# Six layers of local attention: projections in three float32r passes, split weights from the second attention, another order of scores, half copies and a third value buffer

## The chip, the core and the metric

One core of a Trainium2 chip runs one launch of a program that computes a whole four-block network. TensorE (PE, with its weight loads as PEld), VectorE (DVE), ScalarE (ACT), GpSimd (POOL) and SyncE (SP, which here only issues transfers) run their own instruction streams and meet through semaphores. The time is device microseconds of one execution; shown is the median of three runs.

## The reference, cut to what matters

The residual `x` (2048 tokens of 128 features, held with the features on the partitions) passes four blocks, each an attention-like part and a feed-forward part on a normalised copy. The change concerns the feed-forward part of the third block, which is itself a network of six layers. Each layer is:

```python
x = attn_layer(shift_tokens(x), Wqkv[i], q_scale[i], k_scale[i], Wo[i]) + x
x = ffn_layer(shift_tokens(x), ln_g[i], ln_b[i], W1[i], b1[i], W2[i], b2[i]) + x
# attn_layer: 16 heads of 64; attention in windows of 32 tokens, each with the window before it
qkv = x @ Wqkv                       # 128 -> 3 * 1024
q = l2norm(q) * qs ; k = l2norm(k) * ksc      # then rotary tables
out = local_attention(q, k, v) ; return out @ Wo
```

## The kernel before, in words

The program runs stage after stage: block 0 (names b0...), the second attention `b1a` (relative positions; function `attend`), its feed-forward `b1f`, the small attention `b2a`, then the six layers, `b2f` (functions `block2_ffn` and `layers_of_attention`), and block 3 (`b3...`). Between stages all engines meet at a barrier.

In `b2f` the 2048 tokens are 16 tiles of 128 tokens, and six layers make 96 tiles. One loop of steps is written by hand on every engine; step `s` works on four tiles at once. PE does, in this order: the projections of queries and keys of tile `s` (`project_qk`, L2356), the turning of the attention output of tile `s-3` (L2371, `b2f_o_rows`), of the keys and then of the queries of tile `s-1` (L2371), the output product of tile `s-3` (`output`, L2378), the turning of the probabilities of tile `s-2` (L2371, `b2f_prob`), the scores of tile `s-1` (`scores`, L2387 and 128 small products at L2393), the value projection of tile `s` (`project_v`, L2365), a piece of the feed-forward of an earlier quarter (`feed`), and the weighing of the values of tile `s-2` (`weigh_values`, 128 small products at L2406). The feed-forward of a quarter (four tiles) is cut into six phases, one a step, so that steps come in rounds of four. They are called here A (phase 2, L2428), B (phase 3, the three gate products, L2436), C (phases 4 and 0, L2442 and L2417) and D (phases 5 and 1, L2447 and L2422). In steps B the scores stand behind the gate products, directly ahead of the weighing:

```python
gates = any(phase == 3 for f, phase in feed_forward(s))
if not gates and 0 <= s - 1 < n_tiles:
    scores(s - 1, here)
if s < n_tiles:
    project_v(s)
feed(s, range(6))
if gates and 0 <= s - 1 < n_tiles:
    scores(s - 1, here)
if 0 <= s - 2 < n_tiles:
    weigh_values(s - 2, other)
```

ACT copies what PE turned (`b2f_o_cols` L2565, `b2f_kt` L2572, `b2f_qt` L2574, `b2f_pt` L2581), squares queries and keys (`square`, L2527), copies the values (`b2f_v_rows` L2586), does the gelu of the gates in steps B (L2554) and 16 exponentials of 64 columns (L2536). DVE rotates, reduces, normalises the keys (L2649) and scales. POOL adds the rotated parts (L2293, L2296) and takes powers for the lengths (L2303). SP moves the values of a tile across partitions in 16 transfers (L2271 to L2279), behind the weighing of the tile two before it, and in the ninth tile of each layer loads all weights of the next layer into the other of two buffers (L2262). ACT may write the values of a tile into one of two buffers once the transfers of the tile before are done. The projections are float32 products, which stand in a trace as two records each; all of the layer's weights, `b2f_wqkv` among them, come from the inputs.

In `b1a` (`attend`) 16 groups of 8 steps run; ACT copies position scores (L1733) and exponentiates (L1725), SP writes them to a scratch tensor in HBM and reads them back skewed, POOL makes two shifted copies of the keys for each group (L1557).

Of the kernel before, what the change touches and what calls it, by code (L numbers as in the profile page):

```python
# [16 lines left out]
P = 128  # L17
# [557 lines left out]
def block0_ffn(nc, K, w, xn, x):  # L575

    with ExitStack() as ctx:
# [3 lines left out]
        rounded = rounded_constants(M, "b0f", K.pick16, None)  # L581
        parts = two_parts(M, "b0f_xn", [P, N])
        with ExitStack() as inner:
# [3 lines left out]
            to_rows(nc, K, "b0f", probs, ROUTED0, gates, K.pick16[:], rounded)  # L587
# [179 lines left out]
def block0_weights(M, W):  # L767
# [8 lines left out]
              f_router=later("b0f_router", [P, ROUTED0]))  # L776
# [3 lines left out]
def block0_attn(nc, K, weights, xn, x, fetch):  # L780

    with ExitStack() as ctx:
# [18 lines left out]
        with ExitStack() as inner:  # L801
# [4 lines left out]
            rounded = rounded_constants(I, "b0m", K.pick4, 1)  # L806
            parts = two_parts(I, "b0m_flat", [P, N])
            with ExitStack() as rt:
# [3 lines left out]
                to_rows(nc, K, "b0m", probs, 4, gates, K.pick4[:], rounded, b2)  # L812
# [199 lines left out]
def block1_ffn(nc, K, W, w, xn, x, fetch):  # L1012

    with ExitStack() as ctx:
# [7 lines left out]
        rounded = rounded_constants(M, "b1f", K.pick8, 1)  # L1022
        parts = two_parts(M, "b1f_xn", [P, N])
        with ExitStack() as rt:
# [4 lines left out]
            to_rows(nc, K, "b1f", probs, EXPERTS1, gates, K.pick8[:], rounded, b2)  # L1029
# [12 lines left out]
def block2_weights(M, W):  # L1042
# [6 lines left out]
              wqkv=two("wqkv", 3 * INNER), wo=two("wo", PAIRS, P), w1=two("w1", 6, P), w2=two("w2", 3, P),  # L1049
              small=two("small", 9), scales=two("scales", 4, HD2), turn=two("turn", QT, 4, HD2))  # L1050
    return w, first.pairs + layer_weights(W, w, 0)


def layer_weights(W, w, l):
# [3 lines left out]
            ((w.wqkv, of("b2f_wqkv")), (w.turn, W["c_rotary2"]), (w.scales, of("b2f_scales")),  # L1058
# [172 lines left out]
def head_attention(nc, K, W, weights, key, xn, x, relative, fetch=()):  # L1231
# [3 lines left out]
    with ExitStack() as ctx:  # L1235
# [11 lines left out]
        attend(nc, K, key, q_op, k_op, extra, ident, values, table, unseen, merged, relative, fetch)  # L1247
# [179 lines left out]
def attend(nc, K, key, q_op, k_op, extra, ident, values, table, unseen, merged, relative,  # L1427
           fetch):

# [56 lines left out]
    with ExitStack() as ctx:  # L1486
# [13 lines left out]
        if relative:  # L1500
            e_sb = M.sb(f"{key}_e_sb", [P, RING, 2, QW])
            band = M.sb(f"{key}_band", [P, BANDS, 2, BAND])
            e_ps = M.ps(f"{key}_e_ps", [P, QW])
            scratch = K.scratch
        shift_parts = shift_cols[:].rearrange("p t (h c) -> p (t h) c", h=2)[
            :, :, SHIFT_AT:SHIFT_AT + 3 * kinds].rearrange("p n (k r) -> p n k r", r=3)
        with stage(nc, "queries_even", "queries_odd", "keys_even", "keys_odd", "k_kinds", "e_ready", "e_copied",
# [3 lines left out]
                   "merged", "fetched", "dve_chain") as (block, S):  # L1511
# [38 lines left out]
            def _(pool):  # L1550
                if relative:
                    for g in range(GROUPS):
# [162 lines left out]
            def _(act):  # L1715
# [24 lines left out]

                for i in ticks:
                    s, a = i - LAG, i + E_LEAD
                    if 0 <= s < STEPS:
# [7 lines left out]
                    if to_copy_out(i) is not None:  # L1751
                        copy_outputs(to_copy_out(i))

# [423 lines left out]
QK_SCALE = 8.0  # L2177


def block2_ffn(nc, K, W, w, xn, x):  # L2180

    with ExitStack() as ctx:
# [3 lines left out]
        G = Names(  # L2186
            xs=one("xs", B * SEQ), ms=one("ms", B * SEQ),
# [9 lines left out]
            v_rows=two("v_rows", 2, QW), values=two("values", WINS, QW),  # L2197
# [13 lines left out]
def layers_of_attention(nc, K, W, G, Z, xn, x):  # L2211
# [7 lines left out]
    LOADS = 7  # L2219
# [16 lines left out]
    with stage(nc, "began", "weights_even", "weights_odd", "moved_even", "moved_odd",  # L2236
# [6 lines left out]
               "stored", "x_added", "dve_chain") as (block, S):  # L2243
# [11 lines left out]
        def _(sp):  # L2255
# [9 lines left out]
            for g in range(n_tiles):  # L2265
# [770 lines left out]
```

## Time and profile before

| | us |
|---|---|
| runs shown | 3986.25, 3980.16, 3975.45 (median 3980.16) |
| the profiled execution | 3985.77, span 3984.0 from the first to the last instruction |
| PE busy | 3442.9 (86%) |
| DVE, ACT, POOL busy | 2975.4 (75%), 2435.9 (61%), 1397.3 (35%) |
| DMA | 72 GB/s over the span |
| products L2356 of `b2f`, first to last start | 1480.8 to 3232.7 |

A row of the trace is an instruction or a run of like ones: start, length, engine, line, operation, what it writes and reads, shape and count, and in brackets the idle time of the engine before it with what ended it. "issue" means that nothing in the profile explains the wait. A PE row's length counts the fill of the array, so a product's cost is the distance between starts.

### The profile page before, as it was taken

How to read it: one execution, taken by the hardware profiler on the slowest of the kernel's cores; microseconds unless marked ns; L12 is line 12 of the kernel's file. 1: busy time of each engine (PE TensorE's matmuls, PEld its weight loads, DVE VectorE, ACT ScalarE, POOL GpSimd, SP SyncE). 2: the span in 40 equal slices, each digit the busy share in tenths (PEclk: the TensorE clock that was granted, in tenths of full speed). 3: DMA queues.
4: the chain of work that ended last, by engine and by line, in shares of the span. 5: the costliest groups of instructions: out<-in, count | busy, mean ns of one | idle time of the engine just before them, and what ended most of it. 6: DMA issues, size and time to landing. Idle time of an engine off the chain costs nothing. (4 is left out here: it accounts for less than half of the span.)

```text
span 3984.0 us, 102916 instructions
## 1 busy us (share of the span) xinstructions
PE 3442.9 (86%) x40985; PEld 2125.3 (53%) x40985; DVE 2975.4 (75%) x5754; ACT 2435.9 (61%) x4558; POOL 1397.3 (35%) x641
## 2 busy tenths in 40 slices
PE   5668768888859958999999999999999986999898
PEld 3356623333338826666666666666666663222785
DVE  6957657777649868778778778778778755887585
ACT  3436437777728826676676676676676652455573
POOL 4820011111100007666666666666666640000000
PEclk8879859999969979999999999999999997899899
DMA  1000057777511002322322322322322211100000
GB/s 41 0 12 1 14 189 226 232 230 229 179 35 46 11 2 68 100 56 62 97 56 63 96 58 60 97 56 63 96 57 61 59 44 59 35 22 16 13 17 11
DMA packets 174807, 285.80 MB, mean 72 GB/s; under 512 B 36979, under 2 KB 76916, under 8 KB 172404
## 3 DMA queue, kind: packets, MB, share of 16 engines
q1 hardware_dynamic: 173748, 278.48, 23.9%
q8 instruction: 327, 5.36, 0.6%
q14 instruction: 156, 1.28, 0.1%
q10 hardware_dynamic: 576, 0.69, 0.1%
HBM read 104.05 MB, written 74.45 MB: 45 GB/s over the span
## 5 line engine op out<-in xcount | busy, mean ns | idle before, releaser
L2303 POOL TENSOR_TENSOR b2f_norm<-b2f_norm,b2f_minus_half 128x16 f32<-128x16 f32 x192 | 554.8, 2909 | 276.1 <-DVE b2f_norm L2644 276.1
L2293 POOL TENSOR_TENSOR b2f_q<-b2f_q,b2f_q_part 128x1024 f32<-128x1024 f32 x96 | 228.2, 2377 | 656.2 <-DVE b2f_q_part L2634 656.2
L1725 ACT ACTIVATE b1a_weights<-b1a_b_ps 128x512 f32<-128x512 f32 x512 | 278.0, 598 | 39.6 <-PE b1a_b_ps L1650 36.1
L2586 ACT ACTIVATE b2f_v_rows<-b2f_q_ps 128x1024 f32<-128x1024 f32 x96 | 98.4, 1025 | 265.6 <-PE b2f_q_ps L2365 137.5
L1840 DVE TENSOR_REDUCE b1a_tops<-b1a_a_ps 128x1 f32<-128x512 f32 (+3 forms) x512 | 244.8, 502 | 19.7 <-PE b1a_a_ps L1606 18.2
L1557 POOL TENSOR_SCALAR b1a_k_op<-b1a_k_op,b1a_extra 128x1024 bf16<-128x1024 bf16 x32 | 90.6, 2843 | 448.6 <-DMA b1a_k_op<-part_copies 410.3
L1725 ACT ACTIVATE b3a_weights<-b3a_b_ps 128x512 f32<-128x512 f32 (+3 forms) x384 | 161.7, 505 | 136.3 <-PE b3a_b_ps L1660 135.2
L2643 DVE TENSOR_REDUCE b2f_norm<-xn 128x16 f32<-128x1024 f32 x192 | 234.3, 1220 | 13.6 <-ACT xn L2527 5.8
L2536 ACT ACTIVATE b2f_prob<-b2f_odd_ps,b2f_bias,b2f_norm 128x64 f32<-128x64 f32 x768 | 233.2, 443 | 7.5 <-DVE b2f_bias L2660 6.3
L2536 ACT ACTIVATE b2f_prob<-b2f_even_ps,b2f_bias,b2f_norm 128x64 f32<-128x64 f32 x768 | 233.3, 449 | 2.3 <-DVE b2f_bias L2660 2.3
L1733 ACT ACTIVATE b1a_e_sb<-b1a_e_ps 128x512 f32<-128x512 f32 x256 | 153.2, 599 | 123.5 <-PE b1a_e_ps L1592 120.1
L2296 POOL TENSOR_TENSOR b2f_k<-b2f_k,b2f_k_part 128x1024 f32<-128x1024 f32 x96 | 227.4, 2369 | 1.0 <-DVE b2f_k_part L2634 1.0
L2356 PE MATMUL b2f_q_ps<-b2f_wqkv,b2f_xs 128*128 128x512 f32 x384 | 215.4, 688 | 8.1 <-DVE b2f_kt L2610 5.7
L1835 DVE CUSTOM_DVE_ANT_0 b1a_summed<-b1a_a_ps,b1a_band 128x256 f32<-128x256 f32 (+2 forms) x320 | 142.5, 445 | 96.5 <-PE b1a_a_ps L1606 94.5
L2378 PE MATMUL b2f_q_ps<-b2f_o_cols,b2f_wo 128*128 128x128 f32 x1536 | 192.1, 279 | 3.4 <-ACT b2f_o_cols L2565 2.2
L2365 PE MATMUL b2f_q_ps<-b2f_wqkv,b2f_xs 128*128 128x512 f32 x384 | 189.8, 617 | 1.6 <-ACT xn L2527 1.6
L2356 PE MATMUL b2f_k_ps<-b2f_wqkv,b2f_xs 128*128 128x512 f32 x384 | 184.5, 603 | 0.0
L2378 PEld LDWEIGHTS b2f_q_ps<-b2f_o_cols,b2f_wo 128*128 128x128 f32 x1536 | 180.3, 193 | 5.7 <-ACT b2f_o_cols L2565 2.9
L1606 PE MATMUL b1a_a_ps<-b1a_k_op,b1a_q_op 64*128 64x512 bf16 x512 | 139.8, 406 | 23.3 <-DVE b1a_tops L1840 22.9
L2630 DVE TENSOR_TENSOR b2f_q<-b2f_q_ps,b2f_turn 128x1024 f32<-128x1024 f32 x96 | 117.3, 1222 | 51.9 <-PE b2f_q_ps L2356 44.5
L694 POOL TENSOR_TENSOR b0s_drive<-b0s_raw,xn 128x1024 f32<-128x1024 f32 x32 | 135.5, 4233 | 52.0 <-DVE b0s_raw L709 52.0
L2565 ACT ACTIVATE b2f_o_cols<-b2f_even_ps 128x1024 f32<-128x1024 f32 x48 | 49.2, 1026 | 153.8 <-PE b2f_even_ps L2371 153.6
(519 smaller groups left out, 9246.7 us busy)
## 6 DMA issues: line engine op xcount, KB each, us to landing
b2f_values<-b2f_v_rows SPq DMA_DIRECT2D x1534, 64.0 KB
position_scratch<-b1a_e_sb SPq DMA_DIRECT2D x128, 512.0 KB, 3.9
b1a_band<-position_scratch SPq DMA_DIRECT2D x128, 384.0 KB
b2f_wqkv<-in_b2f_wqkv SPq DMA_DIRECT2D x6, 1536.0 KB, 8.2
b2f_turn<-in_c_rotary SPq DMA_DIRECT2D x6, 1024.0 KB, 8.4
b1f_raw<-in_b1f_both SPq DMA_DIRECT2D x9, 512.0 KB, 3.5
part_copies<-b1a_parts SPq DMA_DIRECT2D x12, 256.0 KB
b2f_wo<-in_b2f_wo SPq DMA_DIRECT2D x6, 512.0 KB, 9.7
```

Of the source, the lines that this page charges most:

```text
L1725: act.activation(weights[:, s % P_RING, c, lo:QW], b_room(s, c)[:, lo:QW], ACT.Exp).then_inc(S.exps_ready, 1)
L1733: act.activation(e_sb[:, a % RING, h], e_ps[:], ACT.Copy).then_inc(S.e_copied, 1)
L1835: ins = dve.tensor_tensor_reduce(summed[:, n % 4, 0:z1 - z0], src, band[:, a % BANDS, h, at0:at0 + z1 - z0], 1.0, LOWEST, ALU.add, ALU.max ...
L1840: ins = dve.tensor_reduce(out, src, AX_X, ALU.max)
L2293: pool.tensor_tensor(G.q[:, g % 2], G.q[:, g % 2], G.q_part[:], ALU.add) \
L2296: pool.tensor_tensor(G.k[:, g % 2], G.k[:, g % 2], G.k_part[:], ALU.add) \
L2303: pool.tensor_tensor(part, part, G.minus_half[:, 0:HEADS], ALU.pow) \
L2356: pe.matmul((Z.q, Z.k)[j // 2][:, j % 2], tile_input(g), G.wqkv[:, l % 2, cols(j, QW)], start=True, stop=True).then_inc(S.qk_ready, 1)
L2365: ins = pe.matmul(Z.q[:, h], tile_input(g), wv[:, :, h], start=True, stop=True)
L2378: ins = pe.matmul(Z.q[:, 0, 0:P], G.wo[:, layer(g) % 2, p], G.o_cols[:, p], start=(p == 0), stop=(p == PAIRS - 1))
L2536: act.activation(G.prob[:, i // 2, i % 2], ps[:, i % 2, cols(i // 2, HD2)], ACT.Exp, bias=G.bias[:, i:i + 1], scale=G.norm[:, g % 3, i:i + ...
L2643: chain(dve.tensor_reduce(norm[:, cols(i, HEADS)], G.squares[:, i], AX_X, ALU.add))
```

## The change

In `b2f` each projection becomes three float32r products, head by head, tail by head and head by tail, of inputs and weights that are split into a rounded head and the rest. POOL splits each input tile two steps ahead (`split_tile`). The weights are split beforehand in `b1a`: ACT loads half a layer's weights, POOL splits it, ACT stores both parts to HBM (`wqkv_parts`), 12 halves in the first 12 groups. `b2f_wqkv` now has one buffer with head and tail; the keys' and queries' columns of the next layer are loaded when the last tile of a layer is projected, the values' columns behind that tile's moves. In steps B the scores go ahead of the gate products. The copy of `b2f_o_cols` is made in two halves, each half of the queries' turning waiting for its own half. The values get three buffers. The constants for picking experts are loaded later, with the weights of the blocks that use them.

```diff
-            wqkv=two("wqkv", 3 * INNER), ...
+            wqkv=M.sb("b2f_wqkv", [P, 2, 3 * INNER], F32R), ...
+def projection_weights(K, w, l, lo, hi):
+    return [(w.wqkv[:, part, lo:hi].bitcast(F32), K.wqkv_parts[l, part, :, lo:hi]) for part in range(2)]
...
+                        if g < 2 * LAYERS:
+                            pool.wait_ge((S.raw_even, S.raw_odd)[g % 2], 16 * (g // 2 + 1))
+                            if g:
+                                pool.wait_ge(S.raw_stored, 32 * g)
+                            pool.tensor_copy(raw_parts.head[:], raw[:, g % 2]).then_inc(S.raw_headed, 1)
+                            pool.wait_ge(S.raw_headed, g + 1)
+                            pool.tensor_tensor(raw_parts.tail[:], raw[:, g % 2], raw_parts.head[:].bitcast(F32),
+                                               ALU.subtract).then_inc(S.raw_tailed, 1)
...
                 for i in ticks:
+                    if i >= 0 and i % QT == QT - 1 and i // QT < halves:
+                        store_half(i // QT)
+                        if i // QT + 2 < halves:
+                            load_half(i // QT + 2)
...
             for g in range(n_tiles):
+                ends = g % TILES == TILES - 1 and layer(g) + 1 < LAYERS
+                if ends:
+                    sp.wait_ge(S.qk_ready, 4 * g + 4)
+                    for dst, src in projection_weights(K, G, layer(g) + 1, 0, 2 * INNER):
+                        sp.dma_start(dst, src).then_inc(S.keys_loaded, 16)
                 sp.wait_ge(S.v_copied, g + 1)
...
+                if ends:
+                    for dst, src in projection_weights(K, G, layer(g) + 1, 2 * INNER, 3 * INNER):
+                        sp.dma_start(dst, src).then_inc(S.values_loaded, 16)
...
+            def split_tile(g):
+                l, at = layer(g), at_column(g % TILES)
+                if l:
+                    pool.wait_ge(S.stored, 2 * (g // per_q - QUARTERS + 1))
+                if g >= X_RING:
+                    pool.wait_ge(S.v_ready, g - X_RING + 1)
+                head, tail = (G.x_parts[:, g % X_RING, part] for part in range(2))
+                pool.tensor_copy(head, G.xs[:, at:at + P]).then_inc(S.x_headed, 1)
+                pool.wait_ge(S.x_headed, g + 1)
+                pool.tensor_tensor(tail, G.xs[:, at:at + P], head.bitcast(F32), ALU.subtract) \
+                    .then_inc(S.x_tailed, 1)
...
+            def project(g, ps, weights):
+                head, tail = (G.x_parts[:, g % X_RING, part] for part in range(2))
+                for n, (a, b) in enumerate(((head, 0), (tail, 0), (head, 1))):
+                    ins = pe.matmul(ps, a, weights(b), start=(n == 0), stop=(n == 2))
...
+                    if l:
+                        pe.wait_ge(S.keys_loaded, 16 * PROJECTION_LOADS * l)
+                if g % TILES == 0 and layer(g):
+                    pe.wait_ge(S.values_loaded, 16 * PROJECTION_LOADS * layer(g))
...
-                feed(s, range(6))
                 if gates and 0 <= s - 1 < n_tiles:
                     scores(s - 1, here)
+                feed(s, range(6))
...
-                    act.activation(G.o_cols[:], pairs(here), ACT.Copy).then_inc(S.o_copied, 1)
+                    for j in range(2):
+                        act.activation(G.o_cols[:, 4 * j:4 * j + 4],
+                                       here[:, j].rearrange("p (c n) -> p c n", n=P), ACT.Copy) \
+                            .then_inc(S.o_copied, 1)
...
-                    if s >= 1:
-                        act.wait_ge(moved[(s - 1) % 2], moved_until(s - 1))
+                    if s >= 2:
+                        act.wait_ge(moved[s % 2], moved_until(s - 2))
```

The order of PE in the end of the first step B of `b2f` before (the first row is the turning of the probabilities, the last two rows begin step C):

```order
L2371 MATMUL b2f_even_ps<-c_ident,b2f_prob 128x128 x8
L2365 MATMUL b2f_q_ps<-b2f_wqkv,b2f_xs 128x512 x2
L2436 MATMUL b2f_k_ps<-b2f_normed,b2f_w 128x512 x2
L2436 MATMUL b2f_q_ps<-b2f_normed,b2f_w 128x512
L2387 MATMUL b2f_odd_ps<-b2f_mask,b2f_ident 128x512 x2
L2393 MATMUL b2f_odd_ps<-b2f_kt,b2f_qt 32x64 x64
L2406 MATMUL b2f_even_ps<-b2f_values,b2f_pt 32x64 x64
L2356 MATMUL b2f_q_ps<-b2f_wqkv,b2f_xs 128x512 x2
L2356 MATMUL b2f_k_ps<-b2f_wqkv,b2f_xs 128x512 x2
```

The scores (L2393) and the weighing (L2406) were neighbours. The same place of the changed program, on PE again:

```order
L2450 MATMUL b2f_even_ps<-c_ident,b2f_prob 128x128 x8
L2415 MATMUL b2f_q_ps<-b2f_wqkv,b2f_x_parts 128x512 x6
L2466 MATMUL b2f_odd_ps<-b2f_mask,b2f_ident 128x512 x2
L2472 MATMUL b2f_odd_ps<-b2f_kt,b2f_qt 32x64 x64
L2515 MATMUL b2f_k_ps<-b2f_normed,b2f_w 128x512 x2
L2515 MATMUL b2f_q_ps<-b2f_normed,b2f_w 128x512
L2485 MATMUL b2f_even_ps<-b2f_values,b2f_pt 32x64 x64
L2415 MATMUL b2f_q_ps<-b2f_wqkv,b2f_x_parts 128x512 x6
L2415 MATMUL b2f_k_ps<-b2f_wqkv,b2f_x_parts 128x512 x6
```

The three gate products (L2515) now lie between the scores (L2472) and the weighing (L2485), and two projections are six products.

The transfers that SP issues where the first layer ends, in the changed program: the last two moves of tile 14, then the first moves of tile 15 (in the program before nothing stands between them):

```order
L2322 DMA b2f_values<-b2f_v_rows 32x512
L2326 DMA b2f_values<-b2f_v_rows 32x512
L2316 DMA b2f_wqkv<-wqkv_parts 128x2048 x2
L2322 DMA b2f_values<-b2f_v_rows 32x512
L2330 DMA b2f_values<-b2f_v_rows 32x512
```

The load of the keys' and queries' columns stands behind all moves of tile 14; that of the values' columns (L2335, 128x1024 x2) stands likewise behind all 16 moves of tile 15.

ACT in `b1a`, at the end of the second group, in the changed program (L1744 are exponentials, L1752 copies of position scores):

```order
L1744 ACTIVATE b1a_weights<-b1a_b_ps 128x512 x2
L1752 ACTIVATE b1a_e_sb<-b1a_e_ps 128x512
L1769 DMA wqkv_parts<-b1a_raw_head 128x1536
L1769 DMA wqkv_parts<-b1a_raw_tail 128x1536
L1763 DMA b1a_raw<-in_b2f_wqkv 128x1536
```

Three issues a group came in between the two, in the last step of each of the groups 0 to 9; groups 10 and 11 have the two stores alone, and two loads stand ahead of the first step.

## Rows read from the trace of the kernel before

**Rows 1.** Windows: a layer of b2f; 400 us of b1a (clock, DMA share, GB/s last).

```profile
2350.00:2650.00 300.00, 280.05 (x5247) 191.12 (x5233) 232.77 (x325) 204.22 (x394) 193.20 (x93) 0.98 0.27 71
589.00:989.00 400.00, 356.95 (x2597) 130.20 (x2597) 302.24 (x1030) 306.88 (x580) 67.97 (x24) 0.99 0.72 232
```

**Rows 2.** Timeline of PE in b2f, one round of steps A, B, C, D.

```profile
2350.09 1.98 PE L2356 MATMUL b2f_q_ps<-b2f_wqkv,b2f_xs 128*128 128x512 f32 x4
...
2353.63 1.04 PE L2371 MATMUL b2f_even_ps<-c_ident,b2f_o_rows 128*128 128x128 f32 x8
...
2355.88 1.06 PE L2371 MATMUL b2f_even_ps<-c_ident,b2f_q 128*128 128x128 f32 x8 [0.33 <-ACT b2f_o_cols L2565]
2357.20 2.05 PE L2378 MATMUL b2f_q_ps<-b2f_o_cols,b2f_wo 128*128 128x128 f32 x16 [0.26 <-ACT xn L2527]
...
2362.00 1.98 PE L2365 MATMUL b2f_q_ps<-b2f_wqkv,b2f_xs 128*128 128x512 f32 x4
...
2366.22 1.98 PE L2356 MATMUL b2f_q_ps<-b2f_wqkv,b2f_xs 128*128 128x512 f32 x4
...
2382.96 1.46 PE L2406 MATMUL b2f_even_ps<-b2f_values,b2f_pt 64*32 64x64 f32 x126
2386.68 0.37 PE L2406 MATMUL b2f_even_ps<-b2f_values,b2f_pt 64*32 64x64 f32 x2 [2.26 <-issue]
2386.98 3.33 PE L2356 MATMUL b2f_q_ps<-b2f_wqkv,b2f_xs 128*128 128x512 f32 x4
...
2406.91 1.98 PE L2356 MATMUL b2f_q_ps<-b2f_wqkv,b2f_xs 128*128 128x512 f32 x4
...
2425.49 0.70 PE L2356 MATMUL b2f_q_ps<-b2f_wqkv,b2f_xs 128*128 128x512 f32 x1
```

**Rows 3.** Waits of PE over all of b2f, the longest in total.

```profile
PE b2f_even_ps L2406 <- issue: 54.9, 24, 4.9
```

**Rows 4.** DMA queues in the stretch 2383.9 to 2385.3.

```profile
q8 instruction: 1, 0.02, 5.4%
```

**Rows 5.** Windows: the beginning of that step C (granted clock third from last).

```profile
2386.30:2389.70 3.40, 3.02 (x5) 1.29 (x5) 1.29 (x2) 3.15 (x11) 0.00 (x0) 0.50 0.19 48
```

**Rows 6.** Timeline of PE in b1f: float32r products, thirteen starts, first and last.

```profile
1234.08 0.39 PE L438 MATMUL b1f_h_ps<-b1f_xn_head,b1f_w_head 128*128 128x512 f32 x1
...
1236.80 0.39 PE L438 MATMUL b1f_h_ps<-b1f_xn_head,b1f_w_head 128*128 128x512 f32 x1
```

**Rows 7.** Timeline of ACT in that step B and the following step C.

```profile
2381.61 0.69 ACT L2554 ACTIVATE b2f_hidden<-b2f_q_ps,b2f_small 128x512 f32<-128x512 f32 x1
2382.31 1.28 ACT L2536 ACT_TABLE_LOAD   x1
2384.59 4.86 ACT L2536 ACTIVATE b2f_prob<-b2f_odd_ps,b2f_bias,b2f_norm 128x64 f32<-128x64 f32 x16 [0.99 <-DVE b2f_bias L2660]
2392.93 1.03 ACT L2565 ACTIVATE b2f_o_cols<-b2f_even_ps 128x1024 f32<-128x1024 f32 x1 [3.48 <-PE b2f_even_ps L2371]
```

**Rows 8.** POOL by line and form: a split of 128x128 elsewhere (busy, mean ns).

```profile
L332 POOL TENSOR_TENSOR b1f_bias<-b1f_b,b1f_bias 128x128 fp32r<-128x128 f32 x1 | 0.5, 457 | 0.1
...
L330 POOL CAST b1f_bias<-b1f_b 128x128 fp32r<-128x128 f32 x1 | 0.3, 290 | 44.5 <-SPq L40 44.5
```

**Rows 9.** SP's line of the value moves: the last of one tile's 16.

```profile
2360.39 0.59 SPq L2275 DMA_DIRECT2D b2f_values<-b2f_v_rows  x1
```

**Rows 10.** DMA of the stretch in which a layer's weights load, 2226.4 to 2238.4.

```profile
DMA packets 1079, 3.99 MB, mean 333 GB/s; under 512 B 261, under 2 KB 509, under 8 KB 822
```

**Rows 11.** DMA issues of the whole program: KB each, us to landing.

```profile
b2f_wqkv<-in_b2f_wqkv SPq DMA_DIRECT2D x6, 1536.0 KB, 8.2
```

**Rows 12.** Timeline of PE while those weights load, a step B.

```profile
2237.75 0.85 PE L2406 MATMUL b2f_even_ps<-b2f_values,b2f_pt 64*32 64x64 f32 x36 [4.95 <-issue]
```

**Rows 13.** ACT's DMA issues of the picking constants (min/median/max ns).

```profile
L569 ACTq DMA_DIRECT2D c_pick<-in_c_pick x3: 403/453/461, 0.7 to 1.7; - x3
```

**Rows 14.** DVE's line of the keys' normalisation (min/median/max ns).

```profile
L2649 DVE TENSOR_TENSOR b2f_k<-b2f_k,b2f_norm x96: 1209/1220/1752, 1496.3 to 3250.8; 128x1024 f32<-128x1024 f32 x96
```

More of the change, by code:

```diff
@@ L811, in block0_attn @@
                 keep_top(nc, "b0m", probs, 4, 1)
-                to_rows(nc, K, "b0m", probs, 4, gates, K.pick4[:], rounded, b2)
+                to_rows(nc, K, "b0m", probs, 4, gates, weights.pick4[:], rounded, b2)
             groups = [Names(net=0, select=rounded.pick[:, e],
@@ L1021, in block1_ffn @@
         gates = M.sb("b1f_gates", [P, N], F32R)
-        rounded = rounded_constants(M, "b1f", K.pick8, 1)
+        pick = later("c_pick8", [P, EXPERTS1, P], BF16)
+        rounded = rounded_constants(M, "b1f", pick, 1)
         parts = two_parts(M, "b1f_xn", [P, N])
@@ L1028, in block1_ffn @@
             choose_tokens(nc, w, probs, later.pairs)
-            to_rows(nc, K, "b1f", probs, EXPERTS1, gates, K.pick8[:], rounded, b2)
+            to_rows(nc, K, "b1f", probs, EXPERTS1, gates, pick[:], rounded, b2)
         groups = [Names(net=0, select=rounded.pick[:, e] if e < EXPERTS1 else None,
@@ L1246, in head_attention @@
         project_heads(nc, K, W, weights, key, xn, weights.w, small, q_op, k_op, values, relative)
-        attend(nc, K, key, q_op, k_op, extra, ident, values, table, unseen, merged, relative, fetch)
+        attend(nc, K, key, q_op, k_op, extra, ident, values, table, unseen, merged, relative, fetch,
+               W["b2f_wqkv"] if relative else None)
         merge_heads(nc, K, key, merged, x, weights.w, relative)
@@ L1510, in attend @@
                    "turned_scores", "exps_ready", "out_added", "o_copied", "o_turned",
-                   "merged", "fetched", "dve_chain") as (block, S):
+                   "merged", "fetched", "raw_even", "raw_odd", "raw_headed", "raw_tailed", "raw_stored",
+                   "dve_chain") as (block, S):
             queries, keys = (S.queries_even, S.queries_odd), (S.keys_even, S.keys_odd)
@@ L1752, in _ @@
                         copy_outputs(to_copy_out(i))
+                if halves:
+                    act.wait_ge(S.raw_stored, 32 * halves)
             if not relative:
@@ L2196, in block2_ffn @@
             top=one("top", HEADS), bias=one("bias", HEADS), total=one("total", PAIRS, 2),
-            v_rows=two("v_rows", 2, QW), values=two("values", WINS, QW),
+            v_rows=M.sb("b2f_v_rows", [P, V_RING, 2, QW]), values=two("values", WINS, QW),
             o_rows=one("o_rows", PAIRS, 2, HD2), o_cols=one("o_cols", PAIRS, P),
@@ L2362, in project_v, with turn_rows @@
                     pe.wait_ge(S.y_stored, 2 * (g - 2))
-                wv = G.wqkv[:, layer(g) % 2, 2 * INNER:].rearrange("k (p h d) -> k p h d", h=2, d=HD2)
+                if g % TILES == 0 and layer(g):
+                    pe.wait_ge(S.values_loaded, 16 * PROJECTION_LOADS * layer(g))
+                wv = G.wqkv[:, :, 2 * INNER:].rearrange("k n (p h d) -> k n p h d", h=2, d=HD2)
                 for h in range(2):
-                    ins = pe.matmul(Z.q[:, h], tile_input(g), wv[:, :, h], start=True, stop=True)
+                    ins = project(g, Z.q[:, h], lambda part: wv[:, part, :, h])
                 ins.then_inc(S.v_ready, 1)
-            def turn_rows(rows, ps, done):
+            def turn_rows(rows, ps, done, free=None):
                 for p in range(PAIRS):
+                    if free is not None and p % 4 == 0:
+                        free(p // 4)
                     ins = pe.transpose(ps[:, p // 4, cols(p % 4, P)],
```

77 lines of the change are left out of this document (51 added, 26 removed).

## The prediction

> **What bounds the kernel now.** The page came first: its busy shares and 40 slices put the longest stretch, some 1750 of 3984 us, in the six layers, with PE busy in every slice. The windows of one layer say how much: PE is busy 280.05 of 300 us, DVE 232.77, ACT 204.22, POOL 193.20 [rows 1]. So PE sets the pace there, by products and by few pauses, and the timeline of PE over one round of four steps shows which. A begins at 2350.09, B at 2366.22, C at 2386.98, D at 2406.91, the next A at 2425.49: 16.1, 20.8, 19.9 and 18.6 us, 75.4 a round [rows 2]. A and B differ by 4.7 us. Two float32 products of 512 columns in place of 128-column ones explain under half of it. The rest is a pause of 2.26 us inside the weighing of B, after 126 of 128 records, which nothing in the profile explains ("issue") [rows 2]. The list of waits has it 24 times, 54.9 us in all [rows 3]; there are 24 steps B. In these steps 128 score products stand directly ahead of 128 weighing products, each with a weight load: over 500 instructions in 3 us. The DMA view of 1.4 us in that pause has one transfer, an instruction block on q8 [rows 4]; the wait ends 1.4 us behind that stretch, at 2386.68. I read it as PE running out of instructions. C then begins at a granted clock of 0.50, the 1.2 GHz level, after those sparse products and the pause [rows 5]: its four query records take 3.33 us where A's take 1.98 [rows 2].
>
> The Trainium skill (Runtime: NRT & Kernel Launch, section Instruction fetch mechanics) says that instructions come in 16 KiB blocks and that the fetch is hidden by the pace of issue. The block on q8 fits the first half, the pause speaks against the second. By that rule the pause would have another cause and the new order need not remove it; that is the second rival below.
>
> **The change, part by part.**
>
> Projections. Four of them take from 2350.09 to 2353.63, 0.885 us each [rows 2]. Thirteen float32r products of 512 columns in `b1f` start 2.72 us apart, first to last: 0.227 each, and they too change weights every time [rows 6]. Three are 0.68. A step has six projections and saves 6 x 0.205 = 1.23 us, of it 0.82 ahead of the turns. PE waits for this work and nothing covers it: 4.9 a round.
>
> Half copies. The queries' turning waits 0.33 us for `b2f_o_cols` in A, and the output product then 0.26 for the square of the queries [rows 2]. The first wait goes, but the square comes behind the copy on ACT and behind DVE's rotation, which does not get faster. The bounds are 0 and 1.3 a round; I take half, 0.65.
>
> Order in B. The gate products (2.7 us) now separate scores from weighing, as the value projection and more separate them in C and D, where the round shows no pause in the weighing. The mean pause, 54.9/24 = 2.3, goes [rows 3], and with it the slow start of C, 3.33 - 1.98 = 1.35 [rows 2, 5]. Together 3.65 a round, bounds 0 and 5.
>
> What is late next is ACT. The gelus of B wait for gate products that now end only one weighing (1.46 us [rows 2]) before the end of the step. Behind the last follow a gelu 0.69, a table load 1.28 and 16 exponentials 4.86 [rows 7], 6.83 together. Less the 1.46 that is 5.4, and with an estimated 0.2 for the hand-over ACT is done 5.6 us into C. Now it is done at 2384.59 + 4.86 = 2389.45, 2.5 into C, and copies `b2f_o_cols` at 2392.93, 5.95 into C [rows 7]. Without the slow clock (1.35) and with quicker projections (0.82) that copy could start at 3.8. It starts 1.8 late, and behind it wait the squares, both other copies, hence PE's output product and the scores of C. Loss 1.8 a round, bounds 0 and 1.8.
>
> The sum of a round is 4.9 + 0.65 + 3.65 - 1.8 = 7.4, and 24 rounds give 178.
>
> Boundaries between layers, five. SP ends the issue of the last of a tile's 16 moves at 2360.39 + 0.59 = 2360.98, 10.9 us into a step A [rows 2, 9]. The keys' load of the next layer (2048 KB) is issued behind them in the last step D. A load of 1536 KB lands after 8.2 us [rows 11], and at the 333 GB/s of such a stretch [rows 10] 512 KB more take 1.6: 9.8. It lands 20.7 us into D, while D itself shrinks to about 17 (18.6 - 1.23 - 0.33): PE waits 3.7. The values' load (1024 KB, 8.2 - 1.6 = 6.6) stands behind the 16 moves that begin when D ends: 17 + 10.9 + 6.6 = 34.5. PE, which began tile 16 at 20.7, wants it 11.9 us into a step now, at 2362.00 [rows 2], 10.5 then, at 31.2: it waits 3.3. That is 7 a boundary, 35 in all; with 1.35 of slow clock behind about half of the ten pauses, 41. Bounds: 10 (if the loads land as fast as the stretch's rate alone) and 100 (third rival).
>
> Splitting on POOL. A tile costs 0.29 + 0.457 = 0.75 us [rows 8], at a place in the step where POOL waits for DVE; POOL is busy 193 of 300 us [rows 1]. PE uses the tile two steps later. Nothing, but for 0.75 once at the start; if the cover were gone, 96 x 0.75 = 72. In `b1a` a half is twelve times as wide, at most 12 x 0.75 = 9 us in a group of 33 (24 POOL instructions, two a group, in 400 us), where POOL is busy 67.97 of 400 [rows 1]. Nothing.
>
> The Trainium skill (SBUF — State Buffer, section SBUF: two separate sides) has DVE and GpSimd share a port pair as an exclusive lock, so that a DVE operation with two SBUF inputs waits for all of a GpSimd operation. DVE's normalisation of the keys is such a one and runs while POOL is in its powers, yet its median is 1.220 us, its minimum 1.209 [rows 14]: here the trace does not bear the rule out. By the rule that would be the last rival below.
>
> ACT's transfers in `b1a`. Twelve halves, 36 issues, at 0.453 us of ACT each [rows 13]: 16 us. ACT is busy 307 of 400 us there and PE waits on its exponentials, so little of it is caught up: 0 to 16, I take 14. The transfers add 2.36 MB a group, 7 us at 333 GB/s [rows 10], to a DMA that is busy 0.72 of 33 us [rows 1]: 0.93. Bursts may delay the skewed position scores, which are fetched ahead; 0 to 30, I take 6.
>
> Three value buffers and the smaller load in the ninth tile remove waits on transfers that end behind ACT's and the 4.95 us pause that weights in flight cause [rows 12], which the mean pause above already holds. The picking constants are 640 KB off the first load, 1 to 2 us at 333 GB/s, given back by POOL's first split.
>
> In total 178 - 41 - 20 = 117. The profiled execution took 3985.77, so 3868.8; it lies 5.6 above the median of the runs shown, so **3863 us**.
>
> **The rivals.**
> - *ACT is not late in C.* If the gelus start on the first gates early enough, 24 x 1.8 = 43 stay, and shorter waits at boundaries give 20 more: 3800. For it: ACT has pauses of 3.48 us in C now [rows 7]. Against it: the chain of 6.83 us behind the last gate is serial.
> - *The pause in B is no shortage of instructions.* Then 24 x 3.65 = 88 stay away, but ACT is not late, 43 come back: 3908. Against it stand the place, the count 24 and the block on q8.
> - *Boundaries cost 20 us, not 8.* The loads also hold up instruction blocks, as the 4.95 us with a layer's weights in flight [rows 12]; that delays the last weighing in D, the moves behind it, and the values' load behind those: 3863 + 5 x 13 = 3928.
> - *Slower: `b1a` becomes bound by DMA.* Store bursts from ACT's queue would slow the write and the skewed read on which the scores' maxima wait. To undo the gain each of 12 groups would have to grow by (117 + 20)/12 = 11 us, from 33 to 44; at 14 the time is 4011. Against it: the sum of 0.93 leaves room.
> - *POOL's work holds DVE up.* If DVE stands still for the whole of each split and PE waits for DVE, 96 x 0.75 + 12 x 9 = 180 are lost: 4043. DVE is busy 232.77 of 300 us in a layer and 302.24 of 400 in `b1a` [rows 1], so it has idle time to lose; and the steady 1.2 us of its line beside POOL's powers speaks against it [rows 14].
>
> **How the numbers follow.** Forecast 0.46, first rival 0.20, second 0.12, third 0.11, `b1a` 0.07, port 0.04. A range of 3790 to 3935 holds the first four, 0.89, with room for the bounds of the small terms; alone the forecast spans 3835 to 3895. 0.3%, 12 us, is about what runs of this kernel can tell apart. Faster has 0.89 and part of the `b1a` case, 0.91; within 0.3% 0.03; slower 0.06.
>
> **What would show it.** Right: no pause in the weighing of B, starts of float32r products 0.227 apart, a round near 68 us, ACT the releaser of the queries' turning in C, two waits of 3 to 4 us on DMA at each boundary. Wrong: the 24 pauses of "issue" remain, or move to steps A, where value projection and inverse alone (2.3 us then) separate scores and weighing; PE idle for DVE more than for ACT; a group in `b1a` above 35 us; waits at boundaries of 10 us.

## The result and the profile after

The changed kernel takes 3938.5 us (median of 8 runs, 3922.3 to 3961.3), the kernel before 3982.2 in its 8: a ratio of 0.9892, 95% interval 0.9860 to 0.9924. It is faster by 44 us; 3863 was forecast, with 3935 as the upper end.

The profiled execution is one of the longest of the eight, 3961.15 us with a span of 3959.4; its span is 24.6 us shorter than the one before. Where these come from is read off two lines of PE before and the same two after: the weight loads of the position products in `b1a` and of the output products in `b2f`, each with the first and last start (duration min/median/max ns ahead of them). Before:

```profile
L1592 PEld LDWEIGHTS b1a_e_ps<-b1a_table,b1a_q_op x256: 92/95/114, 544.0 to 1062.6; 64*128 64x128 bf16 x128
...
L2378 PEld LDWEIGHTS b2f_q_ps<-b2f_o_cols,b2f_wo x1536: 186/192/338, 1531.8 to 3284.4; 128*128 128x128 f32 x192
```

After:

```profile
L1611 PEld LDWEIGHTS b1a_e_ps<-b1a_table,b1a_q_op x256: 92/95/148, 549.3 to 1141.8; 64*128 64x128 bf16 x128
...
L2457 PEld LDWEIGHTS b2f_q_ps<-b2f_o_cols,b2f_wo x1536: 186/192/338, 1612.2 to 3262.8; 128*128 128x128 f32 x192
```

`b2f` went from 1752.6 to 1650.6 us, 102.0 less (137 forecast). `b1a` went from 518.6 to 592.5, 73.9 more (20 forecast). The rest (5.3 ahead of `b1a`, 1.2 between the stages, -3.0 behind) makes the 24.6. So three quarters of the gain expected in `b2f` came, and most of it was given back in a stage where only weights are prepared.

**`b2f`.** PE's timeline of one round, as in [rows 2]:

```profile
2458.81 1.67 PE L2415 MATMUL b2f_q_ps<-b2f_wqkv,b2f_x_parts 128*128 128x512 f32 x6
2460.32 1.56 PE L2415 MATMUL b2f_k_ps<-b2f_wqkv,b2f_x_parts 128*128 128x512 f32 x6
2461.72 1.04 PE L2450 MATMUL b2f_even_ps<-c_ident,b2f_o_rows 128*128 128x128 f32 x8
...
2464.84 2.05 PE L2457 MATMUL b2f_q_ps<-b2f_o_cols,b2f_wo 128*128 128x128 f32 x16 [0.20 <-ACT xn L2606]
...
2469.83 1.67 PE L2415 MATMUL b2f_q_ps<-b2f_wqkv,b2f_x_parts 128*128 128x512 f32 x6
2471.34 1.05 PE L2507 MATMUL b2f_k_ps<-c_ident,b2f_inverse 128*128 128x128 f32 x8
...
2473.82 1.67 PE L2415 MATMUL b2f_q_ps<-b2f_wqkv,b2f_x_parts 128*128 128x512 f32 x6
...
2489.10 1.48 PE L2485 MATMUL b2f_even_ps<-b2f_values,b2f_pt 64*32 64x64 f32 x128
2490.51 1.67 PE L2415 MATMUL b2f_q_ps<-b2f_wqkv,b2f_x_parts 128*128 128x512 f32 x6
...
2496.20 1.06 PE L2450 MATMUL b2f_odd_ps<-c_ident,b2f_k 128*128 128x128 f32 x8 [1.74 <-ACT b2f_prob L2615]
...
2509.77 1.67 PE L2415 MATMUL b2f_q_ps<-b2f_wqkv,b2f_x_parts 128*128 128x512 f32 x6
...
2527.86 1.66 PE L2415 MATMUL b2f_q_ps<-b2f_wqkv,b2f_x_parts 128*128 128x512 f32 x6
```

A, B, C and D take 15.0, 16.7, 19.3 and 18.1 us, 69.1 where it was 75.4. The weighing of B (2489.10) runs through, C starts at full pace (its query products take 1.51 us too), and C then waits 1.74 us for the exponentials, at the turning of the keys, which writes the `b2f_odd_ps` that the exponentials still read: 1.8 was forecast, for the queries' turning behind ACT's copy. Six projections take 1.51 + 1.40 + 1.51 = 4.42 us. Over the whole stage, by the starts of the query products, steps B take 78 us less than before, C 21, D 3 and A 1; D and A also carry the boundaries between layers. PE's waits in the whole stage, against the 54.9 of [rows 3]:

```profile
PE b2f_odd_ps L2450 <- ACT b2f_prob L2615: 34.5, 20, 3.1
PE b2f_q_ps L2415 <- DMA b2f_wqkv<-wqkv_parts: 23.1, 8, 4.4
PE b2f_q_ps L2457 <- ACT xn L2606: 19.6, 74, 0.5
...
PE b2f_even_ps L2485 <- issue: 7.7, 6, 2.6
```

**`b1a`.** The windows of 400 us, in the columns of [rows 1] (PE, PEld, DVE, ACT, POOL, clock, DMA share, GB/s):

```profile
606.00:1006.00 400.00, 320.96 (x2170) 116.63 (x2170) 285.39 (x854) 255.63 (x483) 105.97 (x40) 0.91 0.74 248
```

PE, ACT and the number of instructions fell together, to 2170 where 2597 ran, and the granted clock fell from 0.99 to 0.91. The DMA share is 0.74, hardly more than before, and run 4 below has 0.84 at the old pace: the stage is not bound by DMA. The place of the loss stands in the timelines of POOL, DVE, PE and ACT in one group:

```profile
864.91 1.50 POOL L1575 CAST b1a_raw_head<-b1a_raw 128x1536 fp32r<-128x1536 f32 x1 [5.40 <-DMA wqkv_parts<-b1a_raw_tail]
866.50 3.42 POOL L1577 TENSOR_TENSOR b1a_raw_tail<-b1a_raw,b1a_raw_head 128x1536 fp32r<-128x1536 f32 x1
...
865.13 1.35 DVE L1907 TENSOR_TENSOR b1a_shift<-b1a_shift,b1a_shift_cols 128x48 f32<-128x48 f32 x1
866.51 3.50 DVE L1909 CAST b1a_shift_cols<-b1a_shift 128x48 bf16<-128x48 f32 x1
...
865.53 0.39 PE L1625 MATMUL b1a_a_ps<-b1a_k_op,b1a_q_op 64*128 64x512 bf16 x1
870.87 0.61 PE L1625 MATMUL b1a_a_ps<-b1a_k_op,b1a_q_op 64*128 64x512 bf16 x1 [4.95 <-DVE b1a_tops L1881]
...
858.22 0.79 ACTq L1763 DMA_DIRECT2D b1a_raw<-in_b2f_wqkv  x1
859.11 1.09 ACT L1744 ACTIVATE b1a_weights<-b1a_b_ps 128x512 f32<-128x512 f32 x2 [1.15 <-issue]
```

DVE works out the shift of a group in a chain of small operations. While POOL splits 1536 columns (1.50 and 3.42 us, together 4.9), two of them take 1.35 and 3.50 us in place of 0.2: each ends within 0.1 us of POOL's operation. PE waits 4.95 us for the maxima behind the chain, and its next product takes 0.61 in place of 0.39. Earlier in the group ACT lost 1.15 us behind its DMA issues, the last of them L1763 (ACTq is ACT's queue). All operations of three of the chain's lines in this run (min/median/max ns):

```profile
L1895 DVE TENSOR_TENSOR b1a_tops<-b1a_tops,b1a_band x32: 178/190/3384, 583.0 to 1159.1; 128x32 f32<-128x32 f32 x32
L1899 DVE COPY b1a_shift<-b1a_band x32: 165/172/3412, 583.1 to 1159.2; 128x16 f32<-128x16 f32 x32
L1909 DVE CAST b1a_shift_cols<-b1a_shift x32: 236/240/3497, 584.3 to 1160.7; 128x48 bf16<-128x48 f32 x32
```

Before, none of these lines had an operation above 0.25 us (the cast's row reads 236/240/248).

### The profile page after: what moved, and what is told of

The parts are those of the page before. It is cut to its first block and busy times, and to the rows that moved or that the text cites. A ratio compares the mean times of both kernels' runs of the same rounds, so it can differ in the third digit from the quotient of the medians.

```text
span 3959.4 us, 104559 instructions
## 1 busy us (share of the span) xinstructions
PE 3383.0 (85%) x41561; PEld 2245.5 (57%) x41561; DVE 3007.8 (76%) x5754; ACT 2441.5 (62%) x4654; POOL 1514.2 (38%) x857
## 5 line engine op out<-in xcount | busy, mean ns | idle before, releaser
L2415 PE MATMUL b2f_q_ps<-b2f_wqkv,b2f_x_parts 128*128 128x512 f32 x1152 | 328.9, 422 | 39.9 <-DMA b2f_wqkv<-wqkv_parts 23.1
L1744 ACT ACTIVATE b1a_weights<-b1a_b_ps 128x512 f32<-128x512 f32 x512 | 277.2, 596 | 52.2 <-PE b1a_b_ps L1669 37.0
L1752 ACT ACTIVATE b1a_e_sb<-b1a_e_ps 128x512 f32<-128x512 f32 x256 | 153.1, 598 | 184.6 <-PE b1a_e_ps L1611 179.4
L2415 PEld LDWEIGHTS b2f_q_ps<-b2f_wqkv,b2f_x_parts 128*128 128x128 f32 x1152 | 207.4, 193 | 99.1 <-issue 39.0
L1744 ACT ACTIVATE b3a_weights<-b3a_b_ps 128x512 f32<-128x512 f32 (+3 forms) x384 | 161.4, 502 | 137.2 <-PE b3a_b_ps L1679 136.0
L2457 PE MATMUL b2f_q_ps<-b2f_o_cols,b2f_wo 128*128 128x128 f32 x1536 | 198.6, 283 | 21.9 <-ACT xn L2606 19.6
L2415 PE MATMUL b2f_k_ps<-b2f_wqkv,b2f_x_parts 128*128 128x512 f32 x576 | 154.9, 405 | 0.4 <-issue 0.4
L1625 PEld LDWEIGHTS b1a_a_ps<-b1a_k_op,b1a_q_op 64*128 64x128 bf16 x512 | 34.0, 95 | 211.0 <-DVE b1a_tops L1881 140.5
L1640 PE MATMUL b1a_b_ps<-c_ident,b1a_band 128*128 128x128 f32 x704 | 128.8, 303 | 19.1 <-ACT b1a_weights L1744 19.0
```

The source lines that it names most:

```text
L1625: pe.matmul(a_room("tops", a, at)[:, 0:wide], q_op[rows, g % 2, cols(t, P)], k_op[rows, g % K_RING, 0, i * QW:i * QW + wide], start=True, ...
L1744: act.activation(weights[:, s % P_RING, c, lo:QW], b_room(s, c)[:, lo:QW], ACT.Exp).then_inc(S.exps_ready, 1)
L1752: act.activation(e_sb[:, a % RING, h], e_ps[:], ACT.Copy).then_inc(S.e_copied, 1)
L2415: ins = pe.matmul(ps, a, weights(b), start=(n == 0), stop=(n == 2))
L2457: ins = pe.matmul(Z.q[:, 0, 0:P], G.wo[:, layer(g) % 2, p], G.o_cols[:, p], start=(p == 0), stop=(p == PAIRS - 1))
```

## Experiments

The theory is that POOL's long operations hold up DVE operations that read and write SBUF, and PE behind them; the rival, that transfers and their issues slow `b1a`. Stage lengths below are those of the four lines above, from each run's profile; the recorded expectations take longer stretches for the stages (688 us for `b1a` and 1728 for `b2f` in the changed kernel), so compare differences and not lengths. The same code of `b2f` took 1637.2 to 1650.6 us in five profiles (the changed kernel and runs 1 to 4), and the changed kernel has the longest: a difference in `b2f` below some 13 us shows nothing by itself. Ratios are against the kernel before on the same chip; the changed kernel has 0.9892.

**1. No splitting in `b1a`.** Four buffers of unsplit halves, each stored twice:

```diff
-                            pool.tensor_copy(raw_parts.head[:], raw[:, g % 2]).then_inc(S.raw_headed, 1)
...
-                    for part, tile in enumerate((raw_parts.head, raw_parts.tail)):
+                    for part in range(2):
...
-                                      tile[:].bitcast(F32)).then_inc(S.raw_stored, 16)
+                                      raw[:, n % 4]).then_inc(S.raw_stored, 16)
```

> Leaves out POOL's splitting of the weights in b1a: both stored parts hold the unsplit weights; ACT's loads and stores are as many and as large as in the changed kernel. Theory 1 (POOL's two long operations hold DVE's shift chain up, and PE behind it): no DVE operation of that chain over 0.4 us, a group with transfers takes 34 to 35.5 us in place of 41, b1a shrinks from 688 to about 630, the total to 3880 to 3895. Rival (the transfers and their issues on ACT slow b1a): groups stay at 41 us, the total at 3938.

Measured: 3911.0 us, ratio 0.9813 (0.9794 to 0.9833); `b1a` 545.8. The transfers are all there, and 47 of the 74 us are gone: the split is the cause of these. 27 remain. By the medians the split costs 28 us, less than in the profiled execution; the end of the next section offers a reason.

**2. The same split, later.**

```diff
                             if g:
                                 pool.wait_ge(S.raw_stored, 32 * g)
+                                pool.wait_ge(S.less_ready, half * g)
```

> The same work as in the changed kernel; POOL only starts a group's split when DVE has done the shift chain of that group. Theory 1: the shift chain runs at its own 0.2 us an operation, groups take 34 to 36 us, b1a about 630 to 640, the total 3885 to 3900, close to the run without the split. Rival (transfers): 41 us a group and 3938 as before. A third way: the split holds other DVE operations instead, groups of 37 to 40, 3910 to 3930.

Measured: 3908.1 us, ratio 0.9819 (0.9798 to 0.9840); `b1a` 545.0. All the work of the changed kernel, and the time of the kernel without the split, 30 us under the changed kernel. Only the meeting with the shift chain had a price; a total of 3885 to 3900 was too low, since the 27 us stay. The chain's cast is its old self:

```profile
L1910 DVE CAST b1a_shift_cols<-b1a_shift x32: 236/240/245, 579.8 to 1108.6; 128x48 bf16<-128x48 f32 x32
```

**3. The same split in pieces of 128 columns, at the old place.**

```diff
-                            pool.tensor_copy(raw_parts.head[:], raw[:, g % 2]).then_inc(S.raw_headed, 1)
+                            for c in range(12):
+                                piece = cols(c, half_wide // 12)
+                                pool.tensor_copy(raw_parts.head[:, piece], raw[:, g % 2, piece]) \
+                                    .then_inc(S.raw_headed, 1)
...
```

> The changed kernel with each split of 1536 columns done as 12 pairs of operations of 128 columns, at the same place as before. Theory 1a (a DVE operation that is held waits for the POOL operation in progress): no DVE operation of the shift chain is longer than about 0.7 us (0.46 for one piece beside its own 0.2), the eight or so held ones lose 2 to 3 us a group in place of 4.9, groups of 37 to 39, total about 3920. Theory 1b (it waits until POOL has nothing more to do): single operations of 3 to 5 us remain, groups of 41, total 3938.

Measured: 3919.6 us, ratio 0.9858 (0.9836 to 0.9880); `b1a` 552.5. The copy and the cast of DVE's chain:

```profile
L1903 DVE COPY b1a_shift<-b1a_band x32: 164/172/295, 582.5 to 1119.1; 128x16 f32<-128x16 f32 x32
...
L1913 DVE CAST b1a_shift_cols<-b1a_shift x32: 236/240/544, 583.7 to 1120.6; 128x48 bf16<-128x48 f32 x32
```

No operation of the chain is over 0.55 us, and POOL's pieces take 0.29 and 0.45 us: a held operation waits for the one POOL operation in progress. In the groups with halves 33 to 39 us pass, 37 to 39 in four of them.

**4. Transfers on SP.** The later split, its loads and two stores issued by SP in three different steps in place of ACT:

```diff
+                        n, at = group(t - QT)
+                        if t >= QT and n < halves:
+                            if at in (1, 2):
+                                store_half(n, at - 1)
+                            elif at == 3 and n + 2 < halves:
+                                load_half(n + 2)
```

> The later split (as in the run split later, 3908) with the loads and stores of the halves issued by SP in three different steps in place of ACT. Theory (of the 2.2 us a group that are left over the kernel before, 1.3 come from ACT's issues ahead of its exponentials): groups of 34 to 35, b1a 639 to about 622, total about 3890. Rival (the rest is the transfers themselves, and behind one queue with the position scores they delay those more): groups of 37 and more, 3920 and above.

Measured: 3883.0 us, ratio 0.9776 (0.9757 to 0.9795); `b1a` 525.4, where the kernel before has 518.6. The window of 400 us has the work of [rows 1] again (PE 356.95 there), with the DMA share at 0.84:

```profile
606.00:1006.00 400.00, 356.59 (x2608) 130.16 (x2607) 302.62 (x1027) 306.54 (x579) 117.13 (x44) 1.00 0.84 289
```

So of the 27 us some 20 were the issues on ACT, all three in one step ahead of its exponentials; the bytes themselves cost 7 us at most. The edit moves the issues to SP and spreads them over three steps at once; spreading them on ACT was not tried.

**5. The old order in B.**

```diff
-                if gates and 0 <= s - 1 < n_tiles:
-                    scores(s - 1, here)
                 feed(s, range(6))
+                if gates and 0 <= s - 1 < n_tiles:
+                    scores(s - 1, here)
```

> The changed kernel with the scores of a step B behind the gate products again. Theory (PE runs out of instructions where scores and weighing stand together, and ACT is early there): the pause of about 2.3 us in the weighing of B and the slow start of C (1.3) come back, the wait of 1.74 us for ACT in C goes: 24 x (2.3 + 1.35 - 1.74) = 46 more, about 3984; b2f 1728 to 1774. Rival (the order is worth nothing, its gain is given back in C): 3938 within 10.

Measured: 3982.3 us (12 runs), ratio 1.0006 (0.9989 to 1.0024). Without the order the change is worth nothing. The median is 43.8 above that of the changed kernel; in the profile `b2f` takes 1677.7 us, 27.1 more (46 was expected). That profile is of the fastest of the 12 runs, with `b1a` 25 us shorter than in the profile of the changed kernel, so the two figures need not agree. The waits change places as forecast:

```profile
PE b2f_even_ps L2485 <- issue: 47.6, 23, 5.0
...
PE b2f_odd_ps L2450 <- ACT b2f_prob L2615: 4.2, 3, 3.1
```

**6. Gates, scores, values, weighing.** The value projection between scores and weighing in B:

```diff
-                if not gates and 0 <= s - 1 < n_tiles:
+                if gates:
+                    feed(s, range(6))
+                if 0 <= s - 1 < n_tiles:
                     scores(s - 1, here)
                 if s < n_tiles:
+                    if gates:
+                        queries_free_of_ffn(s)
                     project_v(s)
```

> The changed kernel with another order in steps B: gate products, scores, value projection, weighing (ACT does the gelus ahead of the copy of the values). The value projection's 1.5 us now stand between scores and weighing. Theory: no pauses in the weighing of B beyond those of the ninth tile; the gelus start 3 us earlier, so the 1.74 us wait for the exponentials in C shrinks to 0.3 to 0.8: 24 x 1.2 = 29 less, 3909, b2f 1728 to 1700. Rival (a projection of 1.5 us is too little between scores and weighing, or the value projection waits for the third gelu): pauses or waits of 1 us and more appear in B, 3938 or above.

Measured: 3951.0 us, ratio 0.9932 (0.9914 to 0.9951); `b2f` 1659.1. The gain of 29 us did not come, and the interval overlaps that of the changed kernel:

```profile
PE b2f_odd_ps L2450 <- ACT b2f_prob L2619: 30.4, 18, 3.1
...
PE b2f_even_ps L2485 <- issue: 18.8, 16, 3.1
```

The wait in C stays at 1.7 us on the mean, probably since ACT's copy of the values now stands ahead of the exponentials. Of the 18.8 us, 14.7 are five pauses of 2.7 to 3.1 us in ninth tiles, where the next layer's other weights load (the changed kernel has up to 2.6 there). No other pause in a step B is over 0.7 us, where run 5 has mostly 1.4 to 2.3. So outside the ninth tile a value projection of 1.5 us between the two rows of 128 takes most of the pause away, and the 2.7 us of gates take all of it.

**7. Early loads.** The keys' columns between two moves of tile 14, the values' ahead of the moves of tile 15:

```diff
                 if ends:
-                    sp.wait_ge(S.qk_ready, 4 * g + 4)
-                    for dst, src in projection_weights(K, G, layer(g) + 1, 0, 2 * INNER):
+                    sp.wait_ge(S.v_ready, g + 1)
+                    for dst, src in projection_weights(K, G, layer(g) + 1, 2 * INNER, 3 * INNER):
...
                 for h in range(2):
+                    if h and g % TILES == TILES - 2 and layer(g) + 1 < LAYERS:
+                        sp.wait_ge(S.qk_ready, 4 * g + 8)
```

> The changed kernel with the load of the keys' and queries' columns between the eighth and ninth move of tile 14 (behind the last tile's projection still) and that of the values' columns ahead of the moves of tile 15. Theory: the eight waits on these loads at the five boundaries (23 us, and some 4 us of slow clock behind them) go: 3938 - 26 = 3912, b2f 1728 to 1702. Rival: the loads then hold up moves or instruction blocks in the same steps and nothing is won: 3938 within 8.

Measured: 3929.8 us, ratio 0.9868 (0.9846 to 0.9890), whose interval overlaps that of the changed kernel; `b2f` 1627.8, 22.8 less than the changed kernel and 9 less than the shortest of the five, and the wait for `b2f_wqkv` is gone from the list. With the later split:

> The later split and the early loads together. Theory: two independent stages, so the gains add: 3938 - 30 - 23 (b2f measured 1706 with early loads) = 3885 or so.

Measured: 3893.7 us, ratio 0.9796 (0.9779 to 0.9813), `b2f` 1633.0 (1641.5 with the later split alone). The gain here is 8.5 us in the stage and not to be told from none by the ratios (0.9819 without).

**8. Both repairs.** Transfers on SP, the later split and the early loads:

> The later split, its transfers on SP in three steps, and the early loads in b2f together. If the three costs are separate, the gains add: b1a 622, b2f about 1703 (1706 and 1711 with early loads so far), total 3883 - 14 to 20 = 3863 to 3869. If the loads on SP in b1a only gained because something else stood still, or the early loads lose their gain, it stays at 3883.

Measured: 3874.4 us, ratio 0.9722 (0.9707 to 0.9737): the fastest version, 109 us under the kernel before. `b1a` 528.0, `b2f` 1630.9 (1637.2 without the early loads). Here the early loads are told apart by the ratios (0.9776 without them, the intervals do not meet). And with the layer's other weights a tile later:

> The kernel before this one in the list, with the load of the next layer's other weights behind the moves of the tenth tile in place of the ninth, so that it runs at the end of a step C and not through the scores and the weighing of a step B. If instruction blocks come late where that load is in flight, the pauses of 1 to 2.6 us in the weighing of those five steps B (13.1 us in 10 pauses in the profile of later split and early loads, not all of them there) go: 5 to 10 less, about 3858; b2f some 8 less. If those pauses have nothing to do with the load, no change within 5.

Measured: 3880.4 us, ratio 0.9738 (0.9718 to 0.9758): no gain. The pauses in the weighing of those steps B went: three of 1.5 to 1.8 us in ninth tiles in the kernel before it in this list, none over 0.25 us here, and these steps take 5 us less in all. But the wait for the exponentials in C grew from 34.7 to 40.6 us, and two of the steps C in which the load now runs take 21.8 and 21.7 us, where 18 to 19 was usual. So the load does bring the pauses, and what B saves, C waits away.

**9. The projections by themselves**, on the fastest version:

```diff
-                for n, (a, b) in enumerate(((head, 0), (tail, 0), (head, 1))):
-                    ins = pe.matmul(ps, a, weights(b), start=(n == 0), stop=(n == 2))
-                return ins
+                at = at_column(g % TILES)
+                return pe.matmul(ps, G.xs[:, at:at + P], weights(0).bitcast(F32), start=True, stop=True)
```

> The last but one kernel (transfers on SP, early loads; 3874) with each projection as one float32 product of the unsplit input with the rounded heads of the weights; it leaves out the weights' tails, all splitting and transfers stay. It prices the three float32r passes by themselves. By the starts in the changed kernel's trace (six projections 4.42 us, 5.36 before) a step loses 0.94; in C the first four projections (0.63) are hidden in the wait for the exponentials, so a round loses 3.1 and 24 rounds 75: about 3949, b2f 1709 to 1784. By the prediction's 1.23 a step it would be 24 x (4.9 - 0.8) = 98: 3972. If PE waits for DVE or ACT in most steps anyway: 3900 or less.

Measured: 3931.1 us, ratio 0.9881 (0.9857 to 0.9904), 57 above the fastest version; `b2f` 1688.0, 57.1 more. Three passes are worth less than either estimate. PE's wait for the exponentials, in the fastest version and here:

```profile
PE b2f_odd_ps L2452 <- ACT b2f_prob L2617: 34.7, 20, 3.1
...
PE b2f_odd_ps L2450 <- ACT b2f_prob L2615: 21.1, 18, 2.5
```

The wait, 34.7 us with three passes, is 21.1 here: 13.6 of what the passes save is waited away there. By starts 24 x 3.76 = 90 would be saved; another 6 are in smaller waits that are new with three passes (4.2 us in 15 waits of the value projection for DVE's use of the output product, 1.8 for squares). Some 13 us stay unexplained. By the starts of the query products A, B, C and D take 21, 14, 7 and 16 us more in all, where each would take 23 more: A gives nearly all of it, C a third.

## Why the prediction was wrong

The sign held; the time came out 3.5 us above the range. Two steps failed, the split in `b1a` that was put at nothing and the size of the projections' gain; without the split's cost (run 2, 3908) the time would lie in the range, though still 45 us above the forecast. By its steps, on the profiled executions (117 forecast, 24.6 found):

- **Splitting on POOL costs nothing in `b1a`: this step failed**, by 47 us in the profiles and some 30 by the medians (runs 1 and 2). The prediction asked whether POOL had time, which it had, and whether it held DVE up, for which it looked at the keys' normalisation [rows 14], with a median of 1.22 us beside POOL's powers. That was the wrong neighbour: powers of 16 columns do not hold DVE. And it left out the maximum of the same row, 1.752 us. Eight of its 96 operations took 1.35 to 1.75 us, and each of these began 0.04 to 0.13 us behind a copy or a product of POOL; where the POOL copy came second, it was stretched, from a median of 0.40 us to 1.38, ending 0.25 us behind DVE's operation (DVE second in the first pair, POOL in the other):

```profile
2012.33 2.40 POOL L2322 TENSOR_TENSOR b2f_turn<-b2f_turn,b2f_scales 128x256 f32<-128x256 f32 x2
...
2012.40 1.75 DVE L2649 TENSOR_TENSOR b2f_k<-b2f_k,b2f_norm 128x1024 f32<-128x1024 f32 x1
...
2406.30 1.38 POOL L2310 COPY b2f_kt<-b2f_kt 128x256 f32<-128x256 f32 x1
...
2406.21 1.22 DVE L2649 TENSOR_TENSOR b2f_k<-b2f_k,b2f_norm 128x1024 f32<-128x1024 f32 x1
```

  The last rival, at 0.04, had the mechanism. The Trainium skill (SBUF — State Buffer, section SBUF: two separate sides) says that of a GpSimd operation and a DVE operation that needs the shared port pair, such as one with two SBUF inputs, whichever starts first has the pair for its whole length. The traces agree for splits and copies (3.50 us after for a cast that takes 0.24) and not for the powers. The rival's size was wrong: 72 us in `b2f`, where little shows (POOL is mostly the one that waits: its split takes up to 2.38 us in place of 0.46, the DVE line at most 1.28; at the stage's start PE waits 8.6 us for the first split, where it waited 5.7 for DVE before), and 9 us a group in `b1a`, where 4.9 of POOL's work held DVE.
- **ACT's transfers in `b1a`, 14 + 6:** somewhat low. 26 to 27 us remain without the meeting, about 20 of them ACT's issues. The load, last of the three in a group, took 0.92 us of ACT at the median and up to 2.48, where 0.453 was put.
- **Order in B, 3.65, and ACT late in C, -1.8:** right in size, 27 us by profile and 44 by medians where 24 x 1.85 = 44 was forecast. The pauses went but for those of the ninth tile (7.2 of the 7.7 us left), and C waits 1.74. ACT is what C waits for, as forecast, but at the keys' turning, whose buffer the exponentials still read, and not at the queries' turning behind the copy. Of the 24 pauses of [rows 3], 23 lie in steps B; the five long ones in ninth tiles hold 23 of the 54.9 us, so that elsewhere the pause was nearer 1.7 us than 2.3. That the pause is a shortage of instructions fits runs 5 and 6 (it follows how densely the small products stand) and is not shown beyond that.
- **Projections, 4.9 a round: mis-sized.** 24 x 4.9 = 118 was forecast, 57 found (run 9): with the split in `b1a` this is the step that put the time out of the range. The row in `b1f` [rows 6] was a steady stream of one kind. Here six products take 1.40 to 1.51 us, 0.234 each and 0.1 more where they follow other work, so a step saves 0.94 (4.42 in place of 3.54 + 1.82) and not 1.23; and the time saved ahead of the turns is partly waited away, in C above all, since ACT's and DVE's chains did not become shorter. The prediction took all of it as a gain ("PE waits for this work and nothing covers it") and had put the ACT wait against the order alone.
- **Half copies, 0.65 (0 to 1.3):** smaller. PE's waits for `b2f_o_cols` before were 15.0 + 14.2 + 2.2 us in 89 waits, and 1.0 for the squares:

```profile
PE b2f_odd_ps L2371 <- ACT b2f_o_cols L2565: 15.0, 45, 0.5
PE b2f_even_ps L2371 <- ACT b2f_o_cols L2565: 14.2, 42, 0.6
```

  Now 74 waits for the squares take 19.6, and 2.3 are left for the copies: 10.5 us less, 0.4 a round. No run undoes the half copies, the third value buffer or the later constants alone.
- **Boundaries, 41:** somewhat high. Eight waits of up to 4.4 us, 23.1 together (35 forecast); taking them away gave between 6 and 23 us of `b2f`.

The median lies 23 us under the profiled execution, and the meeting in `b1a` can account for that: POOL's split waits for the store of the half before it, so it is a matter of when a store lands. With the split in its old place the stage took 592.5, 589.6, 580.0 and 567.6 us in four profiles (changed kernel, runs 6, 7 and 5), and in these 9, 8, 6 and 4 of the 12 splits held the chain up by 1 us and more: 5.3 to 5.8 us for each above the 545.0 of run 2. A group that misses the chain takes 35 to 37 us, one that meets it 40 to 44. That the runs from 3922 to 3961 differ by this was not tried.

## What to carry to other kernels

Work on an idle engine is free only if it takes nothing that a busy one needs; before a long POOL operation goes beside a chain of small DVE operations in SBUF, look in the trace for a pair of the same kinds that meet (the maximum of a line shows it, its median need not), and order them by a semaphore if they do. Put transfers that can wait on a queue whose engine has nothing urgent behind the issue. And count what a faster product saves only up to the next wait: where another engine ends a step, the saving ends there.

## What the hardware showed unexpectedly

A DVE copy of 128x16 took 3.41 us and a cast of 128x48 3.50 us, against 0.17 and 0.24, while POOL subtracted 1536 columns; reductions and sums that read PSUM ran beside the same work at their usual length. POOL's powers (2.9 us on 16 columns) held no DVE operation: before, 71 of the 96 normalisations of the keys ran beside one, 30 of them wholly, and these 30 have a median of 1.22 us. And 1.5 MB of stores and 0.75 MB of loads a group, issued by SP in three steps ahead of the position scores, cost 7 us in all, where the same three issues in one step of ACT cost 27.
